# Making q, k and v of each head inside the attention loop instead of in a stage ahead of it

## The reference, cut to what matters

```
xn  = layernorm(x)                                  # x: 8 x 2048 x 2048, no scale and shift
qkv = xn @ W_qkv + b_qkv                            # 2048 -> 3 * 2048, 16 heads of 128
att = softmax(where(causal, q @ k.T / sqrt(128), -inf))
ctx = att @ v                                       # per head
y1  = ctx @ W_out + b_out
# a mixture of experts on the same xn: all 8 experts are computed for every token
probs = softmax(xn @ gate_w);  two largest, scaled to sum 1, times alpha[e]  -> combine
y2  = sum_e combine[:, e] * (gelu(xn @ fc1_w[e] + fc1_b[e]) @ fc2_w[e] + fc2_b[e])
out = x + y1 + y2
```

## Time and profile before

| what | value |
|---|---|
| median of 2 runs | 7915.79 us (7855.89 and 7975.69) |
| the profiled execution's own time | 7367.62 us |
| its span, slowest core | 7366.1 us |
| spans of the eight cores | 7351.0 to 7366.1 us |
| TensorE busy, share of the span | 5702.0 us, 77% |
| VectorE, ScalarE, GpSimd busy | 1514.9, 852.9, 549.9 us |
| mean granted TensorE clock | 0.864 |

### The profile page before, as it was taken

One profiled execution on the slowest core, in us unless ns is written; L12 is line 12 of the kernel. 1 busy time (PEld: TensorE's weight loads), 2 busy tenths in 40 slices (PEclk: granted clock), 3 DMA queues, 4 the chain that ended last, 5 costly groups with the idle time before them and its releaser, 6 DMA issues.

```text
span 7366.1 us, 68986 instructions; the slowest of 8 cores (7351.0 to 7366.1 us)
## 1 busy us (share of the span) xinstructions
PE 5702.0 (77%) x25582; PEld 2453.0 (33%) x26065; DVE 1514.9 (21%) x2868; ACT 852.9 (12%) x1651; POOL 549.9 (7%) x696
## 2 busy tenths in 40 slices
PE   2987872444444444649999999999789999999998
PEld 1432331222222221213444444444334444444443
DVE  5011013333333330001112111111111111111111
ACT  1100011232222230000000000000000000000000
POOL 0000000000000000001110111011011111111010
PEclk9987885565556566879999999999899999999999
DMA  3533302000000004357564656555666564656463
GB/s 98 69 52 46 75 29 75 14 23 23 23 23 23 14 15 105 92 146 91 58 81 57 77 61 79 59 72 66 116 105 77 63 75 59 79 62 76 56 82 80
DMA packets 737846, 474.54 MB, mean 64 GB/s; under 512 B 671840, under 2 KB 671984, under 8 KB 727280
## 3 DMA queue, kind: packets, MB, share of 16 engines
q0 software_dynamic: 642544, 310.64, 34.8%
q1 hardware_dynamic: 86000, 125.90, 5.7%
q10 hardware_dynamic: 8976, 33.56, 1.2%
HBM read 696.75 MB, written 75.50 MB: 105 GB/s over the span
## 4 chain that ended last, share of the span: by engine, by line
PE 74%; DVE 9%; issue 7%; DMA 5%; ACT 4%; DVEq 1%; ACTq 0%; another core or an unknown queue 0%; POOL 0%; SPq 0%; POOLq 0%
PE psB L90 39%; PE psA L90 35%; ACT p_sb L90 3%; DVE st L90 2%; DVE p_sb L90 2%; DVE pT_sb L90 2%; DMA ct_sb<-ctxT_d 1%; DMA acc_sb<-out 1%; DMA wo_sb<-w_out 1%; DVE cte_sb L90 1%; DVE psA L90 1%; DVEq L89 1%; DVE o_sb L90 1%; DVE knm_sb L90 0%; ACT hT_sb L90 0%
## 5 line engine op out<-in xcount | busy, mean ns | idle before, releaser
L90 PE MATMUL psA<-xnc_sb,f_sb 128*128 128x512 bf16 x8020 | 1801.6, 380 | 136.8 <-DMA acc_sb<-out 124.1
L90 PE MATMUL psB<-f_sb,hT_sb 128*128 128x512 bf16 x8017 | 1835.4, 384 | 59.5 <-ACT hT_sb L90 48.3
L90 DVE SCALAR_TENSOR_TENSOR acc_sb<-psB,comb_sb,acc_sb 128x1024 f32<-128x1024 f32 x512 | 657.3, 1284 | 3416.7 <-PE psB L90 3416.7
L90 PEld LDWEIGHTS psA<-xnc_sb,f_sb 128*128 128x128 bf16 x8192 | 782.8, 98 | 1139.6 <-issue 232.5
L90 PEld LDWEIGHTS psB<-f_sb,hT_sb 128*128 128x128 bf16 x8192 | 788.1, 99 | 1091.9 <-issue 208.7
L90 ACT ACTIVATE hT_sb<-psA 128x1024 bf16<-128x1024 f32 x256 | 261.9, 1023 | 3692.6 <-PE psA L90 3692.6
L90 PE MATMUL psB<-ident_sb,p_sb 128*128 128x128 bf16 x2176 | 307.4, 299 | 470.0 <-DVE p_sb L90 272.0
L90 POOL DMA_DIRECT2D f_sb<-fc_w x512 | 435.2, 861 | 3139.4 <-PE psB L90 1852.4
L90 ACT ACTIVATE p_sb<-psA,bnd_sb 128x512 bf16<-128x512 f32 (+3 forms) x640 | 398.7, 623 | 1169.6 <-DVE psA L90 519.9
L90 PE MATMUL psB<-pT_sb,vh_sb 128*128 128x512 bf16 (+3 forms) x624 | 215.7, 522 | 241.8 <-DVE p_sb L90 240.8
L90 PEld LDWEIGHTS psB<-ident_sb,p_sb 128*128 128x128 bf16 x2176 | 195.9, 129 | 603.3 <-issue 603.0
(11 more groups left out here) (91 smaller groups left out, 1856.5 us busy)
## 6 DMA issues: line engine op xcount, KB each, us to landing
f_sb<-fc_w POOLq DMA_DIRECT2D x512, 512.0 KB, 12.0
xt_sb<-x SPq DMA_DIRECT2D x16, 1024.0 KB, 5.1
wqk_sb<-w_qkv POOLq DMA_DIRECT2D x32, 512.0 KB, 10.3
x_sb<-x SPq DMA_DIRECT2D x16, 1024.0 KB, 9.1
out<-o_sb SPq DMA_DIRECT2D x16, 1024.0 KB, 5.2
acc_sb<-out SPq DMA_DIRECT2D x2, 8192.0 KB, 40.9
out<-acc_sb SPq DMA_DIRECT2D x2, 8192.0 KB, 27.9
qT_d<-ev_sb ACTq DMA_DIRECT2D x16, 512.0 KB, 8.5
```

Of the source, the lines that this page charges most:

```text
L90: instr = getattr(engine, name)(*a, **kw)
```

## The change

The stages 2 and 3 are gone, and with them `wv_sb`, `ev_sb` and the DRAM copies of q, k and v. `xnT_sb` stays in SBUF during the attention. A function `plan_qkv_head(h)` makes a list of 25 pieces for a head: for each of q, k and v a weight load and four C pieces, then the squares, four column sums with their maxima, the spreading, and four pieces that transpose v back to tokens on the partitions. Head 0's pieces all run ahead of the attention. The pieces of head h+1 are put into the queues during head h, two for each `qbi`, behind the left-over piece and ahead of the scores, so that they are used up in the first half of the fourth group. All C pieces and the norm pieces share one PSUM bank (`ps_qkv`), and the scores now have three banks in turn instead of four. The gate stage and the store of `xnT_sb` follow the attention.

```diff
+        ps_qkv = psA[:, 1536:2048]
+        def plan_qkv_head(h):
+            for role, jb, dest in (("q", h, dest_q), ("k", H + h, dest_k),
+                                   ("v", 2 * H + h, vT_sb[:, :])):
...
+                pieces.append(fill)
+                for cch in range(4):
+                    def mmc(...):
+                        P.wait("tensor", dw, frbox[0])
+                        P.guard_wait("tensor", "psqkv")
+                        def t_qkv(t, wsl=wsl, j0=j0, cch=cch):
+                            for it in range(NI):
+                                t.matmul(ps_qkv[:, 0:512],
+                                         wsl[:, it * 128:(it + 1) * 128],
+                                         xnT_sb[:, it * S + cch * 512:
+                                                it * S + (cch + 1) * 512],
+                                         start=(it == 0), stop=False)
+                            i = t.matmul(ps_qkv[:, 0:512],
+                                         bqkv_row[0:1, j0:j0 + 128],
+                                         ones_row[0:1, 0:512],
+                                         start=False, stop=True)
...
+                            i = sc.activation(
+                                dest[:, cch * 512:(cch + 1) * 512],
+                                ps_qkv[:, 0:512], AF.Copy)
+                        P.set_guard("psqkv", se, se.n)
...
+            for cch in range(4):
+                def knp_c(h=h, cch=cch):
+                    k2_ve = ve.n
+                    P.wait("tensor", ve, k2_ve)
+                    P.guard_wait("tensor", "psqkv")
...
+                        i = vv.reduce_max(knm_sb[0:1, cch:cch + 1],
+                                          ps_qkv[0:1, 0:512], axis=AX.X)
...
+            for pc in plan_qkv_head(0):
+                pc()
+            pendingC = plan_qkv_head(1)
...
             for qbi in range(4):
                 flushB(1)
+                flushC(2)
...
-                    bk = (bank_cur + nb) % 4
+                    bk = (bank_cur + nb) % 3
...
+            if g == 3:
+                if h + 2 < n_h:
+                    pendingC.extend(plan_qkv_head(h + 2))
```

More of the change, by code:

```diff
@@ L343, in build @@
         xnT_ve = ve.n
[L344 to L415, removed]
-                P.on("vector", v_k2)
[L417 to L424, removed]
-                                     start=True, stop=True)
[L426 to L439, removed]
@@ new lines, in build @@
+        ps_S = psA
+        ps_qkv = psA[:, 1536:2048]
+        ps_tr3 = psB[:, 0:1024].bitcast(BF16)
+        ps_ctx = psB[:, 1024:2048]
+        a1s.close()
+        kt_sb = a12.enter_context(nc.sbuf_tensor("kt_sb", [128, 2 * S], BF16))
+        vh_sb = a12.enter_context(nc.sbuf_tensor("vh_sb", [128, 2 * S], BF16))
+        qh_sb = a12.enter_context(nc.sbuf_tensor("qh_sb", [128, 2 * S], BF16))
+        vT_sb = a12.enter_context(nc.sbuf_tensor("vT_sb", [128, S], BF16))
+        p_sb = a12.enter_context(nc.sbuf_tensor("p_sb", [128, 8 * S], BF16))
@@ L443, in build, with v_knb @@
                 P.wait("vector", pe, knb_pe)
-                def v_knb(vv, ps=ps, hh=hh):
-                    i = vv.tensor_copy(kn2b_sb[:, hh:hh + 1], ps[:, 0:1])
+                def v_knb(vv, h=h):
+                    i = vv.tensor_copy(kn2b_sb[:, h:h + 1], ps_qkv[:, 0:1])
                 P.on("vector", v_knb)
[L448 to L456, removed]
@@ new lines, in plan_qkv_head, with flushB, flushC @@
+            return pieces
+        groups = [(h, g) for h in range(n_h) for g in range(4)]
+        pendingB = []
+        pendingC = []
+        def flushB(n):
+            for _ in range(min(n, len(pendingB))):
+                pendingB.pop(0)()
+        def flushC(n):
+            for _ in range(min(n, len(pendingC))):
+                pendingC.pop(0)()
+        if n_h > 0:
+            for pc in plan_qkv_head(0):
+                pc()
+        if n_h > 1:
+            pendingC = plan_qkv_head(1)
@@ L498, in build @@
         P.wait("tensor", d_misc, misc_n)
-        P.wait("tensor", ve, xnT_ve)
+        gcol = lambda k: eg_sb[:, k * 8:(k + 1) * 8]
+        P.guard_wait("tensor", "psqkv")
         def t_ab(t):
-            i = t.matmul(ps_qk[0][:, 0:8], ones_row[0:1, 0:128],
+            i = t.matmul(ps_qkv[:, 0:8], ones_row[0:1, 0:128],
                          alpha_row[0:1, :], start=True, stop=True)
@@ L540, in build @@
             g1_ve = ve.n
-            P.set_guard(f"ps_qk{sl}", ve, g1_ve)
+            P.set_guard("psqkv", ve, g1_ve)
             P.wait("scalar", ve, g1_ve)
@@ L878, in build @@
         p3_pe, p3_ve, p3_se = pe.n, ve.n, se.n
-        a3.close()
+        a12.close()
         a4 = ExitStack()
```

613 lines of the change are left out of this document (316 added, 297 removed).

## The result

| what | before | after |
|---|---|---|
| median of all runs | 7855.89 us (11 runs) | 7484.04 us (12 runs) |
| the profiled execution's own time | 7367.62 us | 7410.35 us |
| span, slowest core | 7366.1 us | 7408.8 us |
| spans of the eight cores | 7351.0 to 7366.1 us | 7365.8 to 7408.8 us |

The ratio after to before is 1.0053 with a 95% interval of 1.0039 to 1.0066: slower by half a per cent, which is within the 2% that count as no change.

A forecast was written before the change was run, and what follows sets the result against it. It took q, k, v as TensorE-bound and the attention as bound by no engine, an almost serial chain. -930 + 860 + 95 = +25 us on 7367.6 gave 7392, ratio 1.0033, carried to 7942 us, range 7720 to 8130.

The forecast's parts named there:

- attention's start: Before the attention only head 0's pieces remain, 69.6 us in sum, so it starts 930 us earlier.
- two pieces of one `qbi`, start to start: In a merged head, 17 matmuls take 3.72 us, then TensorE waits 1.13 us for the copy out of the single bank.
- cold starts a head: Four C pieces a head begin at half clock, 1.9 us each: 7.6 us added, bounds 1.9 and 15.2.
- overlap a head: At three `qbi` of groups 0 and 1 the previous block's chain runs beside the C pieces: -5.9 us.
- given back a head (product with v): C pieces leave TensorE at 2.4 GHz, speeding above all the product with v: -2.5 us, bounds 0 and -5.
- a head's addition: Net time the merged pieces add to each of 15 heads of the attention: 57.3 us, 860 in all.
- end: Gate and store of `xnT_sb` now follow the attention, and the output projection's weights wait for the store: +95 us.
- the exchange: In the attention, the moved q, k and v matmuls are added to the chain, nearly all: +25 us, chance 0.50.
- The rival by which the pieces run under the waits: C pieces fill TensorE's waits in the first two groups: -180 us, 7212 in the trace, ratio 0.979, chance 0.12.
- fell each time: Rival: all eight `qbi` with C pieces start at half clock, nothing given back: +152 us, 7544, ratio 1.024, chance 0.20.
- stayed up: Rival: one cold start in the merged stretch and 5 us given back a head: -123 us, 7269, ratio 0.987, chance 0.13.
- the carry-over: For the whole kernel, the trace's ratio 1.0033 was applied to the two timed runs' median of 7915.8 us: 7942 us.

The follow-up runs named there:

- the thin pieces: The changed kernel with each C piece keeping 1 of its 16 weight tiles, 2 matmuls instead of 17: 6852.2 us.
- the two pairs of experiments that differ by place alone: New pieces behind or ahead of the left-over piece: two per block, changed kernel 7407 against 7210.77 us; one per block, 7307.17 to 7310.00 against 6816.43 to 6820.39.
- the exchanged lines: The changed kernel with the two new pieces of each query block ahead of the left-over piece instead of behind it: 7210.77 us, ratio 0.980 to the kernel before.

## Why the prediction was right, and where it was wrong

By its own steps, core 3 being the slowest of after, and the mean over the eight cores beside it where they differ:

| step | predicted | measured |
|---|---|---|
| attention's start | 238.4 us, -930 | 239.5, -929.0 |
| two pieces of one `qbi`, start to start | 3.72 + 1.13 = 4.85 | 3.87 + 0.96 = 4.83 |
| cold starts a head | 7.6 | 6.7 (mean 5.6) |
| overlap a head | 5.9 | 6.3 less wait for `p_sb` |
| given back a head (product with v) | 2.5 | 2.0 (below) |
| a head's addition | 57.3 | 58.7 (mean 57.6) |
| fifteen heads | +860 | +880.9 |
| end | +95 | +94.8 |
| total in the trace | +25, ratio 1.0033 | +42.7, ratio of runs 1.0053 |
| the stated time | 7942 us, 7720 to 8130 | 7484 median, 7397 to 7409 undisturbed |

**Right: the exchange.** That the 775 us of matmuls would land not in TensorE's idle time but behind it was the core of the forecast, and the wait that stayed (418.0 of 512.8 us), the thin pieces and the two pairs of experiments that differ by place alone show it. The rival by which the pieces run under the waits was the right description of another kernel: the exchanged lines alone gave 7211, beside its 7212. In after it didn't happen. That the two numbers agree within 2 us is luck: the exchanged lines also brought late weights and longer waits at the norm pieces, which that sum didn't have.

**Right: the terms.** The overlap came where it was placed: of the 6.3 us a head, 5.8 went at the three waits behind `qbi` 3 of group 0 (5.15 before, 2.52 after), `qbi` 1 of group 1 (4.70, 3.38) and `qbi` 3 of group 1 (5.39, 3.56), in the head before from 1756 and the one after from 1655. The given-back term can be read from the page's groups, before (first line) and after (second line):

```profile
L90 PE MATMUL psB<-pT_sb,vh_sb 128*128 128x512 bf16 (+3 forms) x624 | 215.7, 522 | 241.8 <-DVE p_sb L90 240.8
```
```profile
L90 PE MATMUL psB<-pT_sb,vh_sb 128*128 128x512 bf16 (+3 forms) x640 | 196.1, 475 | 214.3 <-DVE p_sb L90 213.6
```

522 ns have become 475 in 640 matmuls, 30 us, 2.0 a head. The loss of the fourth score bank was costed at nothing; ScalarE's waits in TensorE are 50.1 us on core 0, which before were 33.3: about 1 us a head that stands in no term. The piece was sized 0.15 us too short and the gap 0.17 too long, which cancel where two pieces follow each other but not in a piece alone: 12 x 0.15 less 4 x 0.17 is 1.1 a head too little. Against these stand cold starts that were 1 to 2 us cheaper. So the match of the sum, to 1.4 us a head on the slowest core, is partly luck: small errors of both signs.

**Right in kind, off in size: the clock.** Cold starts fell only at the four places named, but not each time. Over the fifteen heads q's first and second pieces were long in 29 of 30 cases on every core, k's third and v's second in 13 of 30 (core 0) to 23 of 30 (core 3). So the term of four a head was mis-sized: 2.8 to 3.5. The granted clock of the merged stretch was to be 0.75 to 0.85 and was 0.89 (core 3, from 1661 to 1745), so the first two groups run better than I thought, while the mean over the fifteen heads is 0.74, since the third and fourth group have only the norm pieces and long waits. Neither rival on the clock came: it neither fell each time (at most four long pieces a head, not eight) nor stayed up. On the transposes the trace agrees with what the Trainium skill (TensorE: Matmul & The Clock Gate, Part 4: PE-mode transpose) says, that they don't count as TensorE work for the clock: q's second piece starts at half clock at 1673.78 though TensorE had done transposes ahead of it with gaps of at most 2.2 us. It is no proof, since TensorE also stood idle for about 3 of the 5.6 us before.

**Small misses.** There was to be no wait for `wqk_sb`: it was 1 to 12 us by core, 11.0 on core 3. Q's load was foreseen as barely in time, and that it was. Table loads between copy and exponential: none. One table load stands in the whole attention, at 248.30, where the first exponential follows the first copies. The last head was to take 100 us; it takes 116.6 to the attention's end, as it did before, so that the difference doesn't feel it. And the prediction took all of TensorE's wait for `p_sb` as given by the data, which it is for the transposes alone.

**Wrong: the carry-over.** The step that failed is the one sentence "I carry the ratio over: 7942 us". The trace's own time was 7367.6, the two timed runs 7855.9 and 7975.7, and I named the 7% between them and still took the two runs as the level of the kernel. Neither was at the level that the kernel repeats: over eleven runs that is 7362 to 7366 us, which is where the profiled execution stood; the sum made against it, 7392, is within 18 us of after's 7397 to 7409. The range of 7720 to 8130 was built around the wrong level, so that even a total in the trace just as forecast lay outside it. The 1.5% between the two runs and the agreement of all eight cores in the trace to 15 us, both in the table of times before, should have told which of the two levels was the repeatable one, and the range ought to have reached down to it.

## What to carry to other kernels

In a queue whose instructions run strictly in order, position decides whether filler fills. Independent work has to stand ahead of the instruction that waits, here best one piece of the size of the wait at a time, and it should not itself hand over to the engine that is being waited for. Look first, too, at what the instruction waits for: here half of the wait was for a result that it didn't read. Here the same work placed behind the wait was worth +0.5%, ahead of it in lumps -2.0%, ahead and one at a time (with the narrowed waits) -7.4%, and with the hand-overs kept behind and an early store -8.3%. When a trace and the timed runs differ by several per cent, settle first which level the kernel repeats, before a ratio is carried over.

## What the runs showed of the hardware that I hadn't expected

The eight cores run the same program, and before they agreed to 15 us. After, they differ by 43 us (7365.8 to 7408.8), and 34 of it arise in the attention: the last head starts at 2577.3 on core 0 and at 2611.3 on core 3. One and the same C piece is sometimes short and sometimes long, in different heads on different cores. Summed over the 180 pieces of the fifteen heads, the time above a piece at full clock is 68.9 us on core 0 and 101.0 on core 3, with a mean of 84 over the eight cores. The granted clock at the start of a piece that stands behind a few us of waiting is thus not fixed by the program, and the core with the most cold starts sets the time. In the version with the pieces ahead of the waits the spread is 15 us again (6732.8 to 6747.6), with 38 us of such excess on core 0.
